# A two-layer network with two mixtures of experts on one core: biases added to the slots by exact bf16 products, and fp32 words split by their bits

## The reference

```
def moe_apply(x, combine, dispatch, W, b):
    disp = jnp.einsum('sec,sd->ecd', dispatch, x)
    h = jnp.einsum('ecd,edf->ecf', disp, W) + b[:, None, :]
    return jnp.einsum('sec,ecf->sf', combine, h)

def per_group(xf, lw, lb):
    combine, dispatch = top2_dispatch(xf, Wg, C)
    h = moe_apply(xf, combine, dispatch, W1, b1)     # 128 -> 512
    h = layer_norm(h, lw, lb)
    h = jax.nn.relu(h)
    return moe_apply(h, combine, dispatch, W2, b2)   # 512 -> 128
```

## Time and profile before

| | |
|---|---|
| median of three runs | 424.38 us (422.63, 426.52, 424.38) |
| the profiled execution's own time | 426.38 us |
| its span | 424.6 us |
| granted TensorE clock, mean | 0.955 of full speed |
| busy: PE, DVE, ACT, POOL | 88%, 62%, 48%, 27% |
| chain that ended last | PE 55%, DVE 15%, ACT 8%, issue 8%, DMA 5%, POOL 5% |

### The profile page before, as it was taken

The page is one execution under the profiler, slowest core; times in us unless marked ns, Lnnn a source line. Parts: engine busy times, 40 slices in busy tenths (PEclk is TensorE's granted clock), DMA queues, the critical chain, the costliest instruction groups (busy, mean ns, idle before and its releaser), DMA issues.

```text
span 424.6 us, 7100 instructions
## 1 busy us (share of the span) xinstructions
PE 375.8 (88%) x2668; PEld 213.0 (50%) x2675; DVE 264.9 (62%) x684; ACT 204.9 (48%) x326; POOL 115.9 (27%) x158
## 2 busy tenths in 40 slices
PE   8997968999898999999998899986997999799980
PEld 3665447874344223323233585633854426587860
DVE  4677803325689888898832986527279377771436
ACT  4325102310506676776787586756454453554210
POOL 4011776460505364110010000100000245643142
PEclk9996897999899999999999999999999998899986
DMA  5499714014166562000000000006999576421232
GB/s 118 118 129 309 258 47 120 30 44 114 37 176 173 137 149 78 2 0 3 1 3 0 2 1 2 0 1 234 384 293 289 198 243 199 120 83 41 60 76 62
DMA packets 35877, 46.03 MB, mean 108 GB/s; under 512 B 4778, under 2 KB 21682, under 8 KB 35844
## 3 DMA queue, kind: packets, MB, share of 16 engines
q1 hardware_dynamic: 33156, 38.57, 32.2%
q0 software_dynamic: 2688, 7.02, 5.8%
HBM read 31.67 MB, written 13.78 MB: 107 GB/s over the span
## 4 chain that ended last, share of the span: by engine, by line
PE 55%; DVE 15%; ACT 8%; issue 8%; DMA 5%; POOL 5%; another core or an unknown queue 3%; POOLq 0%; SPq 0%; DVEq 0%; ACTq 0%
PE ps L1491 7%; PE ps L1746 7%; PE ps L1732 6%; PE ps L1707 6%; PE ps L2045 4%; PE ps L1715 4%; PE ps L2074 3%; PE ps L1851 2%; PE ps L1495 2%; DMA R<-h_d,srow 2%; POOL y_d L578 2%; DVE early L1296 2%; PE ps L1860 2%; DVE st L1023 2%
## 5 line engine op out<-in xcount | busy, mean ns | idle before, releaser
L1296 DVE TENSOR_REDUCE early<-ps 128x1 f32<-128x512 f32 x128 | 81.5, 686 | 11.2 <-PE ps L1707 5.9
L804 ACT ACTIVATE R<-ps 128x1024 f32<-128x1024 f32 x64 | 62.7, 1019 | 20.0 <-PE ps L1732 18.9
L1707 PE MATMUL ps<-R 72*128 72x512 bf16 x112 | 38.4, 381 | 1.1 <-DVE early L1296 0.9
L1732 PE MATMUL ps<-R 75*128 75x512 bf16 x128 | 37.4, 379 | 0.1
L648 POOL DMA_INDIRECT R<-h_d,srow x16 | 16.1, 1003 | 72.5 <-DMA h_d<-ff 64.4
L1491 PEld LDWEIGHTS ps<-ident,R 128*77 128x77 f32 (+1 forms) x216 | 24.2, 145 | 23.1 <-issue 9.9
L1491 PE MATMUL ps<-ident,R 128*77 128x128 f32 (+1 forms) x216 | 31.7, 280 | 4.2 <-ACT R L796 1.8
L1746 PE MATMUL ps<-R,vaug 128*9 128x512 f32 x256 | 33.5, 595 | 0.6 <-ACT R L804 0.6
L1495 PE MATMUL ps<-early,ones_b 128*128 128x512 bf16 (+1 forms) x115 | 30.1, 405 | 1.8 <-POOL ident L524 1.6
L1707 PEld LDWEIGHTS ps<-R 72*128 72x128 bf16 x112 | 10.8, 96 | 32.2 <-DVE early L1296 21.9
L1651 PE MATMUL ps<-R 128*128 128x256 f32 x64 | 17.0, 414 | 6.8 <-ACT R L740 6.0
(11 more groups left out here) (341 smaller groups left out, 712.2 us busy)
## 6 DMA issues: line engine op xcount, KB each, us to landing
R<-in_L_ffn_W_dram SPq DMA_DIRECT2D x1, 6144.0 KB, 19.8
h_d<-R SPq DMA_DIRECT2D x12, 256.0 KB, 3.3
q_d<-R SPq DMA_DIRECT2D x24, 96.0 KB, 1.9
R<-k_d SPq DMA_DIRECT2D x24, 96.0 KB
R<-q_d SPq DMA_DIRECT2D x8, 288.0 KB
R<-in_L_ffn_w_dram SPq DMA_DIRECT2D x1, 2048.0 KB
h_d<-ff SPq DMA_DIRECT2D x6, 256.0 KB, 2.9
disp_d<-R SPq DMA_DIRECT2D x1, 1032.0 KB, 12.7
```

The source lines that it names most:

```text
L804: s.activation(probs[idx % 4], ps[:, 2 * (idx % 2):2 * (idx % 2) + 2, :].rearrange("p b t -> p (b t)"), ACT.Exp, scale=QK_SCALE).then_inc( ...
L1296: v.tensor_reduce(mcol[:, u, col:col + 1], bank(ring_bank("row", n)), AX.X, ALU.max).then_inc(s1_max, 1)
L1707: m.matmul(bank(ring_bank("row", n)), Q9[0:KQ, b, h, t * P:(t + 1) * P], K9[0:KQ, b, h, :], start=True, stop=True).then_inc(s1_mm, 1)
L1732: ins = m.matmul(bank(2 * (idx % 2) + j), K9[0:KM, b, h, kt * P:(kt + 1) * P], Q9[0:KM, b, h, :], start=True, stop=True)
```

## The change

1. **Parts by bits.** A new view `top(tile)` reads the upper two bytes of each fp32 word as bf16, in place, with a step of four bytes. It stands in the place of the rounded first and second parts in both mixtures, so ACT's rounding copies go: L718 and L727 (two each), two first parts of the tokens of the second mixture (L874), and L914 and L918 for each tile. In the first mixture the last part is now made by POOL (two subtractions ahead of its scatters), no longer by DVE.
2. **Bias by slot.** A quad's bias is put into its bank by one bf16 product of 96 rows (three exact parts of b1, 24 experts each, at rows 0, 32 and 64) by 512 columns, ahead of its four fp32 products, which now add to it. The weights `of_slot` are 0/1 and say which expert a slot belongs to. For b2 it is six such products of 128 columns ahead of each block's second products. SP loads the biases in three copies by 6 small DMAs in the self-attention, POOL makes the parts behind its work there. The transposed gates, `hidden_bias`, `output_bias`, DVE's `add_bias_rows` and their waits go.
3. **DVE's tile.** The first gathered row times its gate goes to a PSUM bank, the second is added to it from there; rest of the tile as before, and the subtraction of the top view follows the normalizing at once. `hsum` has six buffers, not four.
4. **Second products by chunk.** `second_products(blk, f)` runs all six quads for one chunk f; each waits only for that chunk's evacuation. Block 0 starts when chunk 4 is out. In block 1 two of four chunks go before chunk 15. In block 2 only the last waits for DVE's evacuation of chunk 15.
5. **Order and banks.** The last block's weights are transposed both at once behind group 0, into banks 5 to 7; block 0 goes to banks 6 and 7. ACT copies block 0 (two copies) ahead of the root of tile 6 and evacuates only chunk 8 before the root of tile 7. POOL's `last_rest(0)` and `last_rest(1)` go ahead of the gathers of tiles 2 and 3.

Core of the diff:

```diff
+        def top(tile):
+            return tile.bitcast(BF16).rearrange("p (n two) -> p n two", two=2)[:, :, 1]
...
+            for b in range(B):
+                half = slice(b * TB, (b + 1) * TB)
+                pool.wait_ge(y_rest, b + 1)
+                rest = sent_rest[:, half, :].rearrange("p t d -> p (t d)")
+                g.tensor_tensor(sent_last[:, half, :].rearrange("p t d -> p (t d)"), rest, top(rest),
+                                ALU.subtract).then_inc(y_parts, 1)
...
             def last_rest(u):
-                pool.wait_ge(hid_p2, u + 1)
-                g.tensor_tensor(hparts[u % 6][:, 2, :], hsum[u % 4], hparts[u % 6][:, 1, :], ALU.subtract).then_inc(hid_p3, 1)
+                pool.wait_ge(hid_r1, u + 1)
+                g.tensor_tensor(hlast[u % 6], hrest[u % 6], top(hrest[u % 6]), ALU.subtract).then_inc(hid_p3, 1)
...
                 if q == 2:
                     last_weights()
+                if q in (2, 3):
+                    last_rest(q - 2)
...
-                if q >= 2:
+                if q >= 4:
                     last_rest(q - 2)
...
-            hid_std(4)
-            hid_norm(4)
-            evac_hidden(4)
-            hid_middle(4)
-            evac_hidden(5)
+            evac_hidden(4)
+            hid_std(4)
+            for c in range(5, 8):
+                evac_hidden(c)
             hid_std(5)
...
+            copy_block(0, 0)
+            copy_block(0, 1)
             hid_std(6)
-            hid_norm(6)
-            copy_block(0, 0)
-            hid_middle(6)
-            copy_block(0, 1)
             evac_hidden(8)
-            evac_hidden(9)
             hid_std(7)
-            evac_hidden(10)
-            hid_norm(7)
-            evac_hidden(11)
-            hid_middle(7)
-            for c in range(12, 15):
+            for c in range(9, 15):
                 evac_hidden(c)
...
+                me.link(v.tensor_scalar(partial, got1[q % 4][:, 0, :], g1[:, 0, t:t + 1], None, ALU.mult))
+                me.link(v.scalar_tensor_tensor(out=inner, in0=got1[q % 4][:, 1, :], scalar=g1[:, 1, t:t + 1],
+                                               in1=partial, op0=ALU.mult, op1=ALU.add))
...
+                me.link(v.tensor_scalar(inner, inner, mv[:, q, 0:1], rstd[:, q:q + 1], ALU.subtract, ALU.mult))
+                v.tensor_tensor(rest, inner, top(inner), ALU.subtract).then_inc(hid_r1, 1)
...
+                    quad = i % QUADS
+                    m.matmul(bank(W1_BANKS[i % 3]), of_slot[:, P * quad:P * (quad + 1)], b1_parts, start=True, stop=False)
                     for j in range(4):
-                        e = 4 * (i % QUADS) + j
+                        e = 4 * quad + j
                         ins = m.matmul(ps[32 * j:32 * j + 32, W1_BANKS[i % 3], :], slots1T[:, M1 * e + 32 * blk:M1 * e + 32 * blk + 32], W1[:, e, :],
-                                       start=True, stop=True)
+                                       start=False, stop=True)
...
+            pe.wait_ge(wT_ready, B + 3)
+            second_bias(0)
             pe.wait_ge(ld_W2, 16)
-            second_product(0, 0, 6)
+            for f in range(4):
+                pe.wait_ge(hid1T_ready, 4 + f + 1)
+                second_products(0, f)
             hidden_group(2)
```

More of the change, by code:

```diff
@@ L53 @@
 ATTN0_STEP = 27
-BIAS_BANK = (5, 4, 6, 7, 5, 4, 6, 7)
-BLOCK_BANK = (2, 6, 2)
+PART_BANK = 4
+LAST_BANK = 5
+BLOCK_BANK = (6, 6, 2)
 class Chain:
@@ L486, in _ @@
             load_packed(1, 3)
+            for part in range(3):
+                sp.dma_start(bstage[32 * part:32 * part + E1, 0:F1], a["L1_ffn_b1"]).then_inc(ld_hid, 16)
+                sp.dma_start(bstage[32 * part:32 * part + E1, F1:F1 + D], a["L1_ffn_b2"]).then_inc(ld_hid, 16)
             for u in range(3, UNITS):
@@ L1409, in _ @@
             z = xn
-            def add_bias_rows():
-                for b in range(B):
-                    dve.wait_ge(y1_mm, b + 1)
-                    v.tensor_tensor(half_of(z, b), bank(2 * b), half_of(xn, b), ALU.add).then_inc(y1_dve, 1)
             for i in DVE_QUADS:
@@ L1633, in one_hot_dispatch @@
                             pe.wait_ge(slot_onehot, 2 * (T * c + t + 1))
-                        ins = m.matmul(bank(c), sent_parts[part][:, t, :], pair1h[c][:, t, :, :],
+                        rows = (top(sent[0][:, t, 0:D]), top(sent_rest[:, t, :]), sent_last[:, t, :])[part]
+                        ins = m.matmul(bank(c), rows, pair1h[c][:, t, :, :],
                                        start=(part == 0 and t == 0), stop=(part == 2 and t == T - 1))
@@ L2110, in _ @@
                 dispatch_hidden(gr, f, 1, 2).then_inc(hdisp_mm, 1)
-            second_product(1, 0, 1)
+            for part in range(2):
+                wait_block_copied(pe, 0, part)
+            second_bias(1)
+            for f in range(2):
+                second_products(1, f)
             pe.wait_ge(hid1T_ready, 4 * gr + 1)
```

280 lines of the change are left out of this document (105 added, 175 removed).

## The result

| | before | changed |
|---|---|---|
| median | 423.5 us (422.63, 426.52, 424.38, 421.01) | 427.73 us (426.76, 426.89, 428.57, 431.78) |
| ratio to before | | 1.0163 [1.0089, 1.0238] |
| profiled execution, its span | 426.38, 424.6 | 426.76, 424.8 |
| busy: PE, DVE, ACT, POOL | 88%, 62%, 48%, 27% | 88%, 62%, 45%, 30% |

A forecast was written before the change was run, and what follows sets the result against it. Bound up to 368.68: quads, last copy, landing, POOL; then TensorE with ACT's evacuations at the joints. Group 3 +0.5, the end +1.0, first mixture 0 made +1.5: 427.9 profiled, median 425.9 us, range 420.0 to 431.5.

The forecast's parts named there:

- likeliest case: Whole kernel: time within 1% of before, the forecast as worked out at 425.9 us, chance 0.50.
- Its own signs: Forecast wrong if group 1 is later than 370, chunk 11's pause is absent, or stages before 300 move over 2.
- Bias per quad: Second mixture's quads on TensorE: each added bias product costs 0.45 us, 8.1 for 18.
- dear switch: Rival at the quads: changing between tiled and full products makes a bias cost 0.80; 433 us, half of it 429.5; chance 0.27.
- The landing of block 2: End of the second mixture's quads: the last quad's copy ends at 353.9, 0.3 us later than before.
- Gather of tile 4, group 1: Second mixture: POOL's gather at 360.3; group 1 starts at 367.7, 1.0 us earlier, with POOL's gathers and last parts before it.
- Second bias: Ahead of a block's second products: six bias products take 0.7 us together, bounds 0.3 and 1.2.
- The new wait: Chunk 9's evacuation behind ACT's root of tile 7: TensorE loses 1.9 us before chunk 11, group 3 starts 0.5 later.
- From group 3 to the end: End of the second mixture: two more bias groups, 1.4, less a wait of 0.42 that goes: +1.0 us.
- First mixture: Routing at 31 to 45: DVE's wait of 0.68 goes, POOL's subtractions may slow DVE; taken as 0, bounds -0.7 and +1.7.
- At nothing ... nothing waits for the parts before 326: POOL's part-making and the bias DMAs cost nothing: POOL idles 60.25 us up to 273.97.
- The rival of moving stalls: TensorE's unexplained waits, 5.80 at 65.70 and 1.4 in block 2's last products, may vanish: 418.7 us, chance 0.15.

The follow-up runs named there:

- a_nobias: Changed kernel without the 18 products that put b1 into the quads' banks (b1 missing from the result), on the third chip: 420.75 us, ratio to before 0.9974.
- a_evac9: Changed kernel with ACT's evacuation of chunk 9 ahead of the root of tile 7, on the first chip: 433.47 us, ratio to before 1.0139.
- a_three: Changed kernel with POOL's casts later, chunk 9's evacuation earlier, block 1's rest and block 2 by quads in two parts; second chip: 421.30 us, ratio to before 0.9915.
- a_three2: The same edited kernel as a_three, run again on the third chip: 420.72 us, ratio to before 0.9956.
- b_third: Kernel before, unedited, run again on the third chip: 425.75 us, ratio to before 0.9936.
- a_third: Changed kernel, unedited, run again on the third chip: 423.80 us, ratio to before 1.0018.
- a_slot_late: Changed kernel with POOL's three casts for of_slot moved behind its memsets and iota, some 48 us later, on the first chip: 431.79 us, ratio to before 1.0146.
- a_again: Changed kernel, unedited, run again on the first chip: 434.11 us, ratio to before 1.0186.
- b_again: Kernel before, unedited, run again on the first chip: 426.97 us, ratio to before 0.9959.
- b_bits1: Kernel before with only the changed first mixture (parts by bits, last part on POOL), on the second chip: 423.97 us, ratio to before 0.9926.

## Why the prediction was right, and where not

- **Range and likeliest case.** 427.73 lies in 420.0 to 431.5. The likeliest case was "within 1%", with 0.50; the first measurement says slower by 1.6%, the third chip 0.2%. The terms that the traces bear out are +1.1 for the casts, 0 up to group 3, +1.3 from there and -0.1 in the first mixture's routing, together +2.3; the first mixture's scatters, below, take 0.4 to 1.2 off again, as far as that reaches the end. The forecast was +1.5. The third chip's +1.9 at equal clock agrees with that. So the sum is near for partly other terms than those it was made of, and the 4.2 between the first medians is more than they give: that this time fell in the range is in part luck.
- **Its own signs.** "The forecast is wrong ... if the stages before 300 move by more than 2": they did, by -6.2 and +5.0, and the reasons are not the change's. Taken as a test of the change, this sign was set without knowing how far two executions of one program differ there.
- **Bias per quad**: forecast 0.45, measured 0.47. The dear switch (0.80) is out. The sentence of the Trainium skill ("TensorE: Matmul & The Clock Gate", section on what overlaps and what doesn't) would have given 0.80, so across a change of tiling the trace speaks against it too. (That rival's sum is 425.9 + 6.3 + 1.5 = 433.7, and with half of it 429.8, not 433 and 429.5.)
- **The landing of block 2.** From the one-hots the last quad's copy ends 356.61 - 324.14 = 32.47 later, before 32.23, forecast 32.5. All eight other traces with the bias by slot have 32.46 or 32.47, so this sum is right to a tenth. It does not say that each bias product costs the path 0.47: without all 18 the copy ends only 1.7 earlier (a_nobias), since the quads then wait for their banks, as the prediction said for the case of a cheap bias. (ACT copies 16 of the 18 quads and DVE 2, in both programs, not 15 and 3.)
- **Gather of tile 4, group 1.** From the one-hots, the gather at 37.1 (forecast 38.9, before 38.6), group 1 at 45.4 (forecast 46.3, before 47.3). The size was nearly right; the link was DVE's two tiles on end, not POOL's gathers. On the second and the third chip the gather of tile 4 comes at 37.5 and 37.4 with the old second mixture and at 36.9 to 37.8 with the new one, so its place is unchanged, and before's 38.6 is a longer way from the last copy to the gather. Group 1 came at 46.3 to 48.1 in the four traces of the old one and at 45.4 to 46.1 in the six unedited ones of the new.
- **Second bias**: 0.43 for a group, forecast 0.7.
- **The new wait**: forecast 1.9 ahead of chunk 11 behind the root of tile 7, measured 1.50 there, for that reason. a_evac9 took it away. "The gain before it is eaten here" holds at group 3 (0 in the mean, forecast +0.5), and without the wait the end comes earlier by all of it where no pause falls in (a_three, a_three2).
- **From group 3 to the end**: forecast +1.0, measured +1.3 where no pause falls in, but of other terms. In b_third and a_third the chain of work that ended last leaves TensorE at block 1's last copy and goes on over its store and POOL's fifth gather. That copy ends 11.64 behind group 3 in b_third and 12.03 in a_third: one bias group, not the two (1.4) of the sum less a wait. From it to the fifth gather are 3.0 and 3.5, from there to the end 18.3 and 18.8; why these two are longer no run shows. So the size is right in part by luck. The trace of before had four pauses there, the first one of after none: that difference (-1.4) is not the change's.
- **First mixture**: forecast 0. From DVE's first subtraction (L1221 after) to POOL's first scatter it is 8.95 to 8.97 in three traces with the old code and 8.85 to 8.87 in six with the new. The five others spread from 8.5 to 9.5 (9.40 in the first one of after), the old code's too. So -0.1. The 0.68 of the earlier trace rows went, but 0.42 for TensorE came a little later, and DVE stood idle for TensorE for 1.77 while POOL's two subtractions (2.41 for both) ran: they did not lengthen the routing, and hardly met it. Behind it lies a gain that the prediction does not have: from the first to the last of POOL's 16 scatters of the tokens are 19.8 to 20.6 in the four traces with the old code and 19.4 to 19.5 in all ten with the new.
- **The step that failed: "At nothing ... nothing waits for the parts before 326".** (The range held, this term did not.) It asked who waits for POOL's new work and found nobody. It did not ask what runs on DVE at that moment. The part-making at 212 to 219 indeed cost nothing; the casts at 227.62 fell on the one layer norm for which all engines wait, and cost 1.13 (a_slot_late, and every trace with the casts at that place).
- **The rival of moving stalls** came true in both directions, though not by the program: before's pauses and long first products go with the chip or the time of its runs, its clock with the execution.

**What stays open.** The first measurement (+1.6%) and the first chip (+1.9%, +5.6 ±1.6 at equal clock) say more than the third (+0.2%, +1.9 ±1.0), and the 2.3 of fixed terms are 0.5%. By their intervals these can hardly be one number. In the self-attention a_again took 39.2 against b_again's 36.3, with the clock fallen in one and not the other, but b_third and b_bits1 took more. One further difference runs through all traces of the first chip, in layer 0, whose code is the same: DVE's first subtraction of the first mixture comes at 31.5 in b_again, and at 34.8, 34.0 and 38.9 in a_again, a_slot_late and a_evac9. In the first two of these the granted clock is 0.72 and 0.73 from 20 to 32, in b_again 1.00; in a_evac9 TensorE's products take up to twice as long until 21, though the record of the clock says 1.00 there. On the other chips both sorts occur with the changed program. Whether the changed kernel meets such stretches more often was not settled by one trace for each kernel. b_bits1's 0.7% below before fits the shorter scatters in size only in part.

## What to carry to other kernels

When work moves to an idle POOL, ask also what DVE does while it runs, above all in stretches where one DVE operation holds up every engine; here the same casts 48 us later were free. What is removed from or added to TensorE counts only where its banks are free: 8.5 us of products cost 2 to 4, since the quads waited for their evacuation otherwise. An edit whose gain seems lost may have met a pause that is not its own: look for that row before the gain is called taken back. And two traces of equal length may differ by stretches that cancel: cut them at common points, and take a second chip and a fit against the clock, before a difference of one per cent is given a cause.

## What the runs showed of the hardware

- A bf16 product of the whole array between column-tiled fp32 ones costs 0.47 in place of 0.22, so the switch there and back is some 0.25 (an estimate: 0.47 less the 0.216 of the earlier trace rows).
- Weights and columns read with a step of four bytes cost nothing that can be seen: 36 products of a group take 4.22 with packed parts and 4.22 with two parts by bits as weights; products that stream 512 such columns took 0.39, with packed ones 0.38.
- DVE was not slowed beside POOL when one of its two inputs was in PSUM. DVE over time in the changed kernel, an operation with R and ps as inputs:

```profile
350.94 0.75 DVE L1403 SCALAR_TENSOR_TENSOR t<-R,gate,ps 128x512 f32<-128x512 f32 x1
```

POOL in the same trace ran a subtraction from 350.32 to 351.36 beside it:

```profile
350.32 1.04 POOL L662 TENSOR_TENSOR R<-R 128x512 bf16<-128x512 f32 x1 [3.17 <-DVE R L1411]
```

The same DVE operation takes 0.75 alone. In the earlier trace rows one with two inputs in SBUF took 1.88 beside such a subtraction.
- Runs of one and the same program differ by more than the clock: four traces of one chip and before's first have pauses of TensorE with no releaser, most of 0.3 to 0.45 and some of 0.99, behind POOL's gathers, and 28 to 29 in place of 22 to 25 for one stage of products; the nine traces of the other executions have neither. Whether it is the chip or the time of the runs is open.
